# One kernel, one change: attention's product with the values in two halves, one behind each tile's transposes

## The reference, cut to what matters

```python
# x: (4, 64, 32, 32) float32
x = x + local_attention_7x7(layernorm_over_channels(x))      # stage 1
t = to_tokens(x)                                             # (4, 1024, 64)
h = layernorm(t)
for p in 33 blocks:                                          # stage 2
    op = argmax(h[0, 0, :19])                                # one of 19 weight sets
    q, k, v = h @ wq[op], h @ wk[op], h @ wv[op]
    y = (softmax(q @ k.T / 8) @ v) @ wo[op]
    h = where(attn_mask[op], y, h)
    z = relu(h @ w1[op] + b1[op]) @ w2[op] + b2[op]
    h = where(ffn_mask[op], z, h)
x = from_tokens(t + h)
```

## Time and profile before

| | |
|---|---|
| median of 3 runs | 254.68 us (253.95 to 255.96) |
| the profiled execution | 256.12 us, of which the profiled span is 254.3 us |
| attention section | from about 124 us to 234 us of the span |
| its steady part, tiles 13 to 29 | one pair of tiles every 6.16 us |

### The profile page before, as it was taken

The page is one execution under the profiler, slowest core; times in us unless marked ns, Lnnn a source line. Parts: engine busy times, 40 slices in busy tenths (PEclk is TensorE's granted clock), DMA queues, the critical chain, the costliest instruction groups (busy, mean ns, idle before and its releaser), DMA issues.

```text
span 254.3 us, 5286 instructions
## 1 busy us (share of the span) xinstructions
PE 231.9 (91%) x1814; PEld 158.1 (62%) x1815; DVE 170.4 (67%) x312; ACT 160.3 (63%) x297; POOL 39.5 (16%) x66
## 2 busy tenths in 40 slices
PE   7879972999999999799899999999999999998992
PEld 3346732777787755432375778887777777786330
DVE  0179938677777735464596999897668667761652
ACT  1937754266666694454459988879876666672641
POOL 9900041444445200250000000000000000000000
PEclk9999998599999999799999999999999999999997
DMA  6950000000000001000100000000000000000006
GB/s 162 189 118 3 4 0 1 0 0 3 0 0 0 0 0 31 3 0 10 38 0 0 3 0 0 3 0 3 0 3 3 3 0 3 0 3 0 0 18 149
DMA packets 3302, 4.77 MB, mean 19 GB/s; under 512 B 1041, under 2 KB 2257, under 8 KB 3282
## 3 DMA queue, kind: packets, MB, share of 16 engines
q1 hardware_dynamic: 2758, 3.86, 6.9%
q10 hardware_dynamic: 524, 0.64, 1.1%
HBM read 3.45 MB, written 1.05 MB: 18 GB/s over the span
## 4 chain that ended last, share of the span: by engine, by line
PE 79%; ACT 7%; DVE 7%; issue 4%; DVEq 1%; POOL 0%; ACTq 0%; POOLq 0%
PE ps L613 12%; PE ps L627 11%; PE ps L601 8%; PE ps L451 7%; PE ps L680 6%; PE ps L694 6%; PE ps L483 5%; PE ps L472 5%; ACT arena L903 4%; PE ps L462 2%; PE ps L426 2%; PE ps L345 2%; PE ps L375 2%; PE ps L363 2%; DVE arena L1016 2%
## 5 line engine op out<-in xcount | busy, mean ns | idle before, releaser
L903 ACT COPY arena<-ps 128x1024 f32<-128x1024 f32 x32 | 32.4, 1011 | 20.4 <-PE ps L613 19.3
L1127 DVE TENSOR_REDUCE negmax<-ps 128x1 f32<-128x1024 f32 x32 | 38.7, 1219 | 2.9 <-PE ps L601 2.8
L601 PE MATMUL ps<-h_st,g_st 128*128 128x512 f32 x128 | 38.6, 423 | 0.9 <-DVE h_st L1114 0.5
L852 ACT ACTIVATE pr<-ps,negmax 128x1024 f32<-128x1024 f32 x32 | 35.8, 1119 | 4.2 <-DVE negmax L1127 3.9
L613 PE MATMUL ps<-eye,pr 128*128 128x128 f32 x256 | 33.7, 275 | 2.8 <-ACT arena L903 2.3
L613 PEld LDWEIGHTS ps<-eye,pr 128*128 128x128 f32 x256 | 28.6, 140 | 11.1 <-issue 5.1
L627 PE MATMUL ps<-arena,vk 128*64 128x128 f32 x512 | 31.5, 276 | 1.1 <-ACT arena L903 1.1
L627 PEld LDWEIGHTS ps<-arena,vk 128*64 128x64 f32 x512 | 27.6, 137 | 3.8 <-issue 2.3
L786 ACT ACTIVATE prob<-ps,negmax 128x308 f32<-128x308 f32 x32 | 16.3, 513 | 21.0 <-DVE negmax L1027 21.0
L601 PEld LDWEIGHTS ps<-h_st,g_st 128*128 128x128 f32 x128 | 21.8, 188 | 9.0 <-issue 3.2
L1137 DVE TENSOR_SCALAR pr<-pr,rinv 128x1024 f32<-128x1024 f32 x32 | 24.1, 753 | 1.1
(11 more groups left out here) (112 smaller groups left out, 335.3 us busy)
## 6 DMA issues: line engine op xcount, KB each, us to landing
arena<-in_key_onehot SPq DMA_DIRECT2D x4, 361.0 KB, 6.1
out<-tabs SPq DMA_DIRECT2D x8, 128.0 KB, 2.3
x<-in_x SPq DMA_DIRECT2D x2, 256.0 KB, 3.8
x<-in_x ACTq DMA_DIRECT2D x2, 256.0 KB, 5.1
w1d<-in_ffn_w SPq DMA_DIRECT2D x4, 64.0 KB, 2.2
w2p<-in_ffn_pack SPq DMA_DIRECT2D x2, 65.5 KB, 2.1
spread_w<-in_spread_mat SPq DMA_DIRECT2D x4, 32.0 KB, 5.1
mean_w<-in_mean_mat SPq DMA_DIRECT2D x1, 96.0 KB, 2.0
```

The source lines that it names most:

```text
L601: mm = nc.tensor.matmul(ps[:, 2 * h + c, :], g_st[:, b2, h, q0:q0 + P], h_st[:, b2, h, part, c * 512:c * 512 + 512], start=(part == 0), st ...
L852: nc.scalar.activation(pr[:, n % 2, :], ps[:, 2 * (n % 2):2 * (n % 2) + 2, :], ACT.Exp, bias=negmax[:, 0, n % 2:n % 2 + 1], accum_out=rows ...
L903: nc.scalar.copy(prt[:, n // 8 % 2, n % 2, :, q0:q0 + P], ps[:, 4:6, :].rearrange("p b (c q) -> p (b c) q", c=4)).then_inc(S["s_pt"], 1)
L1127: nc.vector.tensor_reduce(negmax[:, 0, n % 2:n % 2 + 1], ps[:, 2 * (n % 2):2 * (n % 2) + 2, :], mybir.AxisListType.XY, ALU.max, negate=Tru ...
```

## The change

`mix(j)` gets a second argument. `mix(j, 0)` makes key chunks 0 to 3 and holds the waits, `mix(j, 1)` makes chunks 4 to 7 and raises `s_pv` where it did. `mix(j, 0)` stands behind the transposes of tile 2j+3, where the whole product stood, and `mix(j, 1)` behind those of tile 2j+4. `mix(14)` and `mix(15)` stay whole. No instruction is added to or taken from any other engine.

```diff
-                def mix(j):
+                def mix(j, half):
 
                     g, cols = j // 4, slice(j % 4 * P, j % 4 * P + P)
-                    pe.wait_ge(S["s_pt"], base + 2 * j + 2)
-                    if j == 8:
-                        pe.wait_ge(S["vo_copied"], 3 * a + 3)
-                    if j % 4 == 0 and j > 0:
-                        pe.wait_ge(S["h_ready"], chunks + 4 + g)
-                    for c in range(NKC):
+                    if half == 0:
+                        pe.wait_ge(S["s_pt"], base + 2 * j + 2)
+                        if j == 8:
+                            pe.wait_ge(S["vo_copied"], 3 * a + 3)
+                        if j % 4 == 0 and j > 0:
+                            pe.wait_ge(S["h_ready"], chunks + 4 + g)
+                    for c in range(4 * half, 4 * half + 4):
                         for h in range(2):
                             mm = nc.tensor.matmul(ps[C * h:C * h + C, 7, cols],
                                                   vk[:, g // 2, c, C * h:C * h + C],
                                                   prt[:, g % 2, h, c, cols],
                                                   start=(c == 0), stop=(c == NKC - 1))
-                    if j % 4 == 3:
+                    if j % 4 == 3 and half == 1:
                         mm.then_inc(S["s_pv"], 1)
...
                     if n == NT - 1:
-                        mix(14)
+                        mix(14, 0)
+                        mix(14, 1)
                     tile_turn(n)
-                    if 3 <= n < NT - 1 and n % 2 == 1:
-                        mix((n - 3) // 2)
+                    if 3 <= n < NT - 1:
+                        mix((n - 3) // 2, (n - 3) % 2)
...
-                mix(15)
+                mix(15, 0)
+                mix(15, 1)
```

## The result

| | before | changed |
|---|---|---|
| median | 254.56 us (6 runs, 253.95 to 256.15) | 258.79 us (6 runs, 257.37 to 259.39) |
| the profiled execution | 256.12 us, span 254.3 | 258.44 us, span 256.6 |
| attention, first transposes (tile 0) to the first matmul of the feed-forward section | 134.03 to 234.17: 100.14 us | 132.77 to 236.48: 103.71 us |

What follows compares the result with a forecast made beforehand. It took the attention section to be bound by TensorE's work plus its standstills. Terms -4.05 + 4.55 + 2.0 + 0.5 + 1.0 + 0.5 = +4.5 moved the median from 254.68 to 259.2 us, range 256.2 to 261.4.

Steps and rivals of the forecast that it cites:

- nine gaps closed: Steady part from tile 13: odd transposes no longer wait for ScalarE's copy of the even tile; 9 x 0.45, -4.05 us.
- thirteen seams: Thirteen more runs of product matmuls on TensorE, each paying 0.16 on entering and 0.19 on leaving: 13 x 0.35, +4.55 us.
- store(2) at tile 27: store(2) waits for the later mix(11, 1) ahead of normalise(27) on VectorE; tile 27's transposes wait 1.5 to 1.6 us.
- its echo at the scores of tile 30: Behind the late normalise, maxima(28) and ScalarE's exponential come late, so scores of tile 30 wait another 0.4 us.
- queries at n = 4 and 6: Queries come 1.03 later behind mix(0, 1) and mix(1, 1), delaying tiles 6 and 8: 0.5 each, +1.0 us.
- tile 12: VectorE's queue, with store(0) between odd and even tile, makes tile 12 some 0.5 us late, bounds 0 and 0.8.
- the end: Behind tile 29's transposes stands 1.03 of product instead of 1.90, so tile 30 waits for VectorE: +0.5 us.
- Rival 1: The seam's entry belongs to the semaphores, so second halves enter free: 2.1 less, +2.4, 257.1 us; chance 0.13.
- Rival 2: No additional seam on entry or exit, but TensorE waits on VectorE: +1.0, 255.7 us, no measurable change; chance 0.09.
- rival 3: Only the closed gaps remain, the cut product no dearer and VectorE's queue absorbing store(2): -3.5, 251.2 us; chance 0.04.
- the steady part: From tile 13 on, closed gap and added seam nearly cancel: a pair of tiles takes 6.07 us against 6.16.
- Rival 4: VectorE becomes the bound between odd and even tile; eight pairs lose 0.3 each: +7, 261.7 us; chance 0.11.

Runs made afterwards that it cites:

- experiment 5: Kernel before, whole products, ScalarE's copy of even tiles in two halves, the next odd tile's first four transposes waiting for the first only: 251.05 us, ratio 0.9862, section 96.75.
- experiment 3: Kernel before with one further 128x128 transpose, result unused, in the middle of each of mix(7) to mix(13): 258.45 us, ratio 1.014, section 102.98.
- experiment 7: Changed kernel with only mix(6) to mix(10) cut, other products whole where they stood before: 254.31 us, ratio 0.996, section 99.60.
- Experiment 1: Changed kernel with store(2) moved from tile 26 to tile 27 in VectorE's order: 256.38 us, ratio 1.0074, section 101.91.
- experiment 6: Changed kernel with store(2) at tile 27, queries and values ahead of the half product, mix(13) whole behind tile 29: 255.23 us, ratio 1.0032, section 100.94.
- experiment 8: Kernel before with even tiles' copies and tile 31's in halves, the last one's first half releasing mix(15)'s first four chunks: 251.67 us, ratio 0.9869, section 96.34.

## Why the prediction was right

It forecast +4.5 us; the medians differ by 4.2, the section by 3.6. The account by its own steps, in the section. Where two tiles are named, the time is from the transposes of the one to those of the other; "free" is the distance where nothing waits, 3.02 for one tile and 6.05 for two.

| term | forecast | measured | from |
|---|---|---|---|
| nine gaps closed | -4.05 | about -4.0 | 0.44 a pair in experiment 5 |
| thirteen seams | +4.55 | about +4.3 | 13 x (0.14 + 0.19): halves 1.02 + 1.02 against 1.90, scores 1.12 against 0.93 |
| store(2) at tile 27 | +1.55 | +1.4 | tile 25 to 27: 7.46, free 6.05 |
| its echo at the scores of tile 30 | +0.4 | +0.4 | tile 27 to 29: 6.45, free 6.05 |
| queries at n = 4 and 6 | +1.0 | +0.7 | tile 5 to 6 and 7 to 8: 0.57 and 0.56 over free; before 0.14 and 0.32 over its own 3.92 |
| tile 12 | +0.5 | +0.2 | tile 11 to 13: 6.26, free 6.05 |
| the end | +0.5 | +0.3 | tile 29 to 30: 2.34, against 2.89 before less the 0.88 that moved |
| scores of tile 6 | 0 | +0.25 | tile 3 to 4: 3.27, free 3.02 |
| sum | +4.5 | +3.6 | |

**The gap and what fills it: right.** Experiment 5 removes it in another way and finds the period that the rows of before gave, 5.71 for 5.72.

**The seams: right, in cause and nearly in size.** Rival 1 (the entry belongs to the semaphores) would have had 14 pauses on entering; there are 28, and experiment 3 makes the same pause where nothing waits. Rival 2 (no seam) falls with the same rows, and rival 3 with them and with the stall at `store(2)`. That the steady part would gain almost nothing (6.07 for 6.16) was 6.04 to 6.06, and experiment 7 has it by itself. One reading was too wide: the prediction has the pause of 0.17 "at every change of shape and none elsewhere", but the change from 128*128 to 128*1 for the transpose of a row is in the same trace, without a pause. The sum has no such change in it.

**The stall at store(2): right.** Experiment 1 takes back 1.80 of the 1.95 that the two terms had.

**The queries: right in cause, a third too large.** The forecast took 0.5 for each of tiles 6 and 8; it was 0.43 and 0.24, as tile 8 already lost 0.32 before the change.

**Tile 12 and the end: the sizes were off.** The forecast took VectorE to be 1.3 ahead of TensorE at tile 11, a lead stepped through eleven tiles, and had tile 12 late by 0.5; it was 0.2. The end was worked out as 2.5 against 1.9, which is 0.6, and taken as 0.5; experiment 6, which has `mix(13)` whole, gives back 0.35 there (tile 29 to 31: 5.78 for 6.13).

**The scores of tile 6 were left out.** The stall is small, and other terms were too large by more, so the sum hides it.

**Rival 4** (VectorE the bound in the steady part) did not come: from tile 15 to 25 no matmul of the transposes waits.

So the mechanism was right, and against the section the forecast was 0.9 too large. That the medians differ by 4.2, nearer to 4.5, is no sign that the terms were better than this table says: the interval of the ratio, 2.7 to 5.0 us, holds both 3.6 and 4.5 and can't tell them apart.

## What to carry to other kernels

A product with 64-column weights between groups with 128-column weights has a price for entering and leaving, 0.29 to 0.35 us here, and it was the same for half a product as for a whole one. Before such a group is cut up to fill a gap, set that price beside the gap: 0.45 here, so that a tenth of a microsecond a pair was left, and the stalls that the changed order brought to the queues behind it cost far more. The same gap was worth 3.4 us when ScalarE's copy, for which TensorE waited, was cut instead. And an instruction that waits on a moved end (`store(2)`) has to move with it.

## What the runs showed of the hardware that was not expected

- The pause between 128*64 and 128*128 weights is there without any semaphore, and for a single instruction (experiment 3): one transpose in the midst of a product took 0.26 instead of 0.11 and made the rest of the product 0.15 dearer.
- The price of leaving depended on what followed: 0.15 for a transpose, 0.19 for 512-column scores.
- A transpose with 128*1 weights had no pause behind 128*128 weights, and 0.17 behind 128*64.
- A copy of 128x1024 in two halves cost ScalarE 1.07 instead of 1.01 (experiment 8), so cutting it was nearly free:

```profile
223.25 1.07 ACT L914 COPY arena<-ps 128x512 f32<-128x512 f32 x2 [0.42 <-PE ps L617]
```
